# One attention layer and its feed-forward: scores in four 64x64 tiles, and V before the output projection

## What is computed

```python
q = _l2norm(proj(Wq)); k = _l2norm(proj(Wk)); v = proj(Wv)        # 16 heads of 16
attn = einsum('bhqd,bhkd->bhqk', q, k)
mask = (rel < 0) | (rel >= WINDOW)                                # rel = key - query, WINDOW = 128
attn = softmax(attn + where(mask, -1e30, -abs(rel) * slope_of_head))
out  = einsum('bte,de->btd', einsum('bhqk,bhkd->bhqd', attn, v), Wo)
x = _layernorm(x + out)
x = _layernorm(x + ffn(x))         # 256 -> 1024 -> 256, weights binarised per row, exact gelu
```

## Time and profile before

| what | us |
|---|---|
| median of 3 runs | 373.69 (373.42 to 374.68) |
| the profiled execution, its own time | 373.84 |
| its span in the trace | 372.1 |
| TensorE busy | 358.0 (96%) |
| VectorE busy | 318.2 (86%) |
| ScalarE busy | 310.0 (83%) |
| GpSimd busy | 274.5 (74%) |

### The profile page before, as it was taken

How to read it: one execution, slowest core, us unless ns; L and a number is a source line. 1 busy time by engine, 2 the same in 40 slices (tenths; PEclk the granted TensorE clock), 3 DMA queues, 4 the chain that set the end, 5 groups by cost and what they waited for, 6 DMA issues and landing times.

```text
span 372.1 us, 11965 instructions
## 1 busy us (share of the span) xinstructions
PE 358.0 (96%) x3933; PEld 243.9 (66%) x3933; DVE 318.2 (86%) x856; ACT 310.0 (83%) x539; POOL 274.5 (74%) x418
## 2 busy tenths in 40 slices
PE   8699999999999999999999999999999999999991
PEld 5445567766766776676676667775666666666671
DVE  3967789998898988888998997869789999999995
ACT  3579789888898898898899999887888888887873
POOL 1169999899999999999999999857554754754321
PEclk9989999999999999999999999999999999999998
DMA  6757944564464446467676754303303404404113
GB/s 225 147 80 173 193 93 117 105 121 87 111 124 101 111 100 127 100 156 162 132 140 143 160 106 82 58 3 60 58 0 58 114 18 98 114 17 97 58 57 113
DMA packets 99490, 38.31 MB, mean 103 GB/s; under 512 B 84736, under 2 KB 98432, under 8 KB 99328
## 3 DMA queue, kind: packets, MB, share of 16 engines
q1 hardware_dynamic: 99456, 37.89, 46.7%
HBM read 12.72 MB, written 4.19 MB: 45 GB/s over the span
## 4 chain that ended last, share of the span: by engine, by line
PE 62%; DVE 24%; issue 5%; DMA 4%; SPq 2%; ACT 1%; DVEq 1%; POOL 0%; POOLq 0%
PE ps L392 14%; PE ps L402 13%; PE ps L435 9%; PE ps L372 8%; PE ps L411 6%; DVE prob L1150 4%; DVE w L1150 4%; PE ps L532 4%; PE ps L419 3%; DVE zstats L1170 3%; DVE resid L1198 3%; PE ps L566 2%; PE ps L426 2%; DVE z L1160 2%; SPq L273 2%
## 5 line engine op out<-in xcount | busy, mean ns | idle before, releaser
L1363 POOL TENSOR_SCALAR_AFFINE_SELECT prob<-prob 128x512 f32<-128x512 f32 x252 | 154.4, 648 | 14.0 <-ACT prob L673 13.4
L673 ACT ACTIVATE prob<-ps 128x1024 f32<-128x1024 f32 (+1 forms) x128 | 122.2, 1009 | 11.6 <-PE ps L372 11.5
L402 PE MATMUL ps<-wqkv,xt 128*128 128x512 f32 x124 | 60.4, 610 | 1.4 <-DVE qkn L934 1.1
L532 PE MATMUL ps<-yT,sgn 128*128 128x512 f16 x256 | 61.1, 379 | 0.0
L745 ACT ACTIVATE ps<-ps,bias,alpha 128x512 f32<-128x512 f32 x64 | 47.9, 750 | 15.6 <-PE ps L532 12.5
L1431 POOL TENSOR_TENSOR resid<-z,resid 128x256 f32 (+1 forms) x31 | 22.6, 728 | 46.0 <-DVE z L1160 46.0
L392 PE MATMUL ps<-prob,vdiag 128*17 128x128 f32 x1024 | 51.4, 274 | 0.0
L392 PE MATMUL ps<-prob,vnext 128*17 128x128 f32 x992 | 50.0, 273 | 0.0
L372 PE MATMUL ps<-qkT 64*128 64x256 f16 (+1 forms) x512 | 38.8, 270 | 2.1 <-DMA qkT<-parts 2.1
L532 PEld LDWEIGHTS ps<-yT,sgn 128*128 128x128 f16 x256 | 25.0, 98 | 22.6
L435 PE MATMUL ps<-wo,oT 128*128 128x256 f32 x128 | 36.2, 405 | 0.0
(11 more groups left out here) (115 smaller groups left out, 679.8 us busy)
## 6 DMA issues: line engine op xcount, KB each, us to landing
xt<-in_xT SPq DMA_DIRECT2D x32, 128.0 KB, 2.1
resid<-in_x SPq DMA_DIRECT2D x32, 128.0 KB, 2.2
out_dram<-resid SPq DMA_DIRECT2D x7, 512.0 KB, 2.9
w<-in_w2T SPq DMA_DIRECT2D x1, 1024.0 KB, 8.1
w<-in_w1T SPq DMA_DIRECT2D x4, 256.0 KB, 3.3
w_nat<-in_w SPq DMA_DIRECT2D x4, 256.0 KB, 3.6
wqkv<-in_wqkvT SPq DMA_DIRECT2D x3, 256.0 KB, 4.1
qkT<-parts SPq DMA_TRANSPOSE x32, 4.3
```

The lines of the kernel that those rows point to most:

```text
L402: mm = nc.tensor.matmul(ps[:, QK[slot % 2], :], xt[:, slot, k, :], wqkv[:, k, 0:2 * D], start=(k == 0), stop=(k == DC - 1))
L532: mm = nc.tensor.matmul(ps[:, bank, :], sgn1[:, c, P * k:P * k + P], yT[:, par, a, c, :, :], start=(m == 0), stop=(m == 2 * DC - 1))
L673: nc.scalar.activation(to, scored, ACT.Exp, scale=QK_SCALE ** -2).then_inc(exp_done, 1)
L1363: return nc.gpsimd.affine_select(out=at, in_=at, compare_op=ALU.is_ge, fill=0.0, base=-near, pattern=[[0, CH], [1 if near else -1, P]], ch ...
```

## The change

The scores of a chunk were 4 products of 64 rows by 128 keys with 256 queries. They are now 8 products of 64 rows by 64 keys, each with the 192 queries that those keys can be seen by; the parts of PSUM that are never written are zeroed once at the start. For this the queries of two neighbouring blocks must lie side by side, so `qkT` is laid out anew with a fifth place, and every fourth block's queries are transposed a second time by a DMA of half the size. The order of the probability slots changes with it. In the steps 4 to 28 TensorE projects V right after the first scores, and projects the output after q and k. VectorE follows: sums of squares first, then the residual addition and the layer-norm statistics, then the values. ScalarE's logarithm now waits for the layer-norm statistics of the same step (`ln_seed`), where before VectorE's `half<-ss` carried this wait and the statistics stood ahead of it. The first four residual rows are loaded in two pairs, and a few statements at the start of the feed-forward change places (left out below).

```diff
--- before.py
+++ after.py
...
-OWN_AT, NEAR_AT = (0, 4, 1, 5), (2, 3)
+
+OWN_AT, NEAR_AT = (2, 3, 4, 5), (0, 1)
...
-        qkT = sb("qkT", [P, XS, 2 * (H // 2), P], F16)
+
+        qkT = sb("qkT", [P, 2 * (H // 2), XS + 1, P], F16)
...
-                sp.dma_start_transpose(qkT[:, QSLOT[s]],
+                sp.dma_start_transpose(qkT[:, :, s, :],
                                        parts[:, s % 2].rearrange("p h a d -> p (h a d)")).then_inc(qk_in[s % 2], 16)
+                if s == 0 and not (isinstance(n, int) and n == 0):
+                    sp.dma_start_transpose(qkT[:, 0:H // 2, XS, :],
+                                           parts[:, 0, 0:H].rearrange("p h a d -> p (h a d)")).then_inc(again_in, 16)
...
+            for n in range(2):
+                sp.dma_start(resid[:, n, :], x[n]).then_inc(first_resid[0], 16)
             turn_parts(XS, 0)
-            for n in range(XS):
-                sp.dma_start(resid[:, n, :], x[n]).then_inc(first_resid, 16)
+            for n in range(2, XS):
+                sp.dma_start(resid[:, n, :], x[n]).then_inc(first_resid[1], 16)
...
+                queries_at = (slot - 1) * P if slot else (XS - 1) * P
+                windows = ((0, P + P // 2), (P // 2, 2 * P)) if both else ((P, P + P // 2), (P, 2 * P))
                 for t in range(2):
+                    rows_of_queries = qkT[:, 2 * c + t].rearrange("p s q -> p (s q)")
                     for hp in range(2):
                         row = slice(64 * hp, 64 * hp + 64)
-                        queries = qkT[row, first:last + 1:last - first, 2 * c + t, :] if both else qkT[row, here, 2 * c + t, :]
-                        mm = nc.tensor.matmul(ps[:, SC + 2 * (c % 2) + hp, 2 * P * t:2 * P * t + wide],
-                                              qkT[row, here, H // 2 + 2 * c + t, :], queries,
-                                              start=True, stop=True)
+                        for half, (first, last) in enumerate(windows):
+                            keys = slice(P // 2 * half, P // 2 * half + P // 2)
+                            at = queries_at if both else -P
+                            mm = nc.tensor.matmul(ps[keys, SC + 2 * (c % 2) + hp, 2 * P * t + first:2 * P * t + last],
+                                                  qkT[row, H // 2 + 2 * c + t, slot, keys],
+                                                  rows_of_queries[row, at + first:at + last],
+                                                  start=True, stop=True)
                 mm.then_inc(s_done, 1)
...
-            def project_v(n, slot):
+            def project_v(n, slot, added=None):
 
                 count(pe, v_ready, n)
-                count(pe, resid_done, n - 4)
+                count(pe, resid_done, n - 4 if added is None else added)
...
-                if out:
+                full = out and next1 and next3
+                if full:
+                    project_v(i + 1, (slot + 1) % XS, i - 4)
+                elif out:
                     project_out(i - 4, i + 1)
                 if strips:
                     turn_strips(i - 3)
...
+                if full:
+                    project_out(i - 4, i + 1)
                 if before_rows:
                     before_rows()
                 if strips:
                     turn_rows(i - 3)
-                if next1 and next3 and not early:
+                if next1 and next3 and not full and not early:
                     project_v(i + 1, (slot + 1) % XS)
...
             def norm_of(i, next3, ln):
                 base, cols = norm_base(i, next3), norm_columns(next3, ln)
-                if not next3:
+                if ln:
                     act.wait_ge(ln_seed, i - 3)
...
-            def sums_of(n, ln):
+            def sums_of(n):
...
-                if ln:
-                    dve.wait_ge(ln_seed, n - 6)
...
-                if out and next3:
-                    add_output(i - 4)
...
                     y_row(i - 5, prev3)
+                if next3:
+                    sums_of(i + 3)
+                    if out:
+                        add_output(i - 4)
                 if ln:
                     layer_norm(i - 4)
                 if amid:
                     amid()
-                if next3:
-                    sums_of(i + 3, ln)
-                    if not double_first:
-                        fade_values(i + 1, (slot + 1) % XS)
+                if next3 and not double_first:
+                    fade_values(i + 1, (slot + 1) % XS)
...
             nc.vector.memset(ps[:, OT, :], 0.0).then_inc(consts, 1)
+            nc.vector.memset(ps[:, SC:SC + 4, :], 0.0)
...
-            dve.wait_ge(first_resid, 16 * XS)
             step(4, 0, prev_ln=False)
+            dve.wait_ge(first_resid[1], 16 * 2)
```

60 lines of the change are left out of this document (35 added, 25 removed).

## The result

| | before | after |
|---|---|---|
| median us | 373.56 (4 runs, 373.27 to 374.68) | 382.94 (4 runs, 382.64 to 383.26) |
| the profiled execution, span in the trace | 373.84, 372.1 | 383.13, 381.3 |
| TensorE busy | 358.0 (96%) | 354.7 (93%) |
| VectorE busy | 318.2 (86%) | 321.6 (84%) |
| ScalarE busy | 310.0 (83%) | 312.1 (82%) |

The change makes the kernel 2.5% slower: the ratio is 1.0251, 95% interval 1.0226 to 1.0276. The forecast was 377.4 us with a range up to 381.6. The direction came out, the size did not: 9.4 us where 3.7 were expected.

What follows compares the result with a forecast made beforehand. TensorE bounds the kernel before; afterwards a chain through several engines (7.53 us, 7.48 per step with relief) does. 373.84 + 4.7 - 0.7 - 0.3 = 377.5 profiled, median 377.4 us, range 370.0 to 381.6.

Steps and rivals of the forecast that it cites:

- The scores: TensorE's score products, four tiles at a time: 0.08 us less per pair of chunks, 0.16 per step.
- The logarithm's chain: Exps, GpSimd's masks and low halves, `half<-ss`, addition, statistics, logarithm, next exps: closes at 7.53 us, above TensorE's 7.18.
- It stays held: VectorE's `half<-ss` cannot start before 157.33, so it still waits for GpSimd's low-halves instruction of 157.07 to 158.23.
- The second chain: V opens the step and waits for the previous step's values: a stall up to 0.3 us, not counted again.
- The relief of one step in four: GpSimd's low halves come a chunk earlier there: 0 to 0.43 us less in four steps, giving 7.48 per step.
- The wait for `oT`: TensorE's weighted sums wait for ScalarE's copy of the transposed rows: about 0.08 us per step.
- Outside the loop: Scores in seven other steps, counted as 0.7 us less, and paired first residual loads in step 4, 0.3 less.
- rival D: Second transposing DMA arrives late every fourth step by some 0.5 us: +3, total 380.4 us; chance 0.08.
- Rival B: Score tiles' column halves run in turn on TensorE: pair 0.75 us, step 7.68, total 384.8; chance 0.08.
- A: `half<-ss` is not held and runs in 0.18 us: TensorE's 7.18 is the step, total 370.3; chance 0.17.
- C: `half<-ss` is held only on every second step: mean step 7.33 us, total 373.9; chance 0.12.
- The rule against the scores: Skill's minimum of about 25 ns between product starts: 16 products take 0.40 us, not 0.32; gain per pair 0.03.

Runs made afterwards that it cites:

- The square: Changed kernel (382.94 us) against it with V's values made early (375.60), with the logarithm not waiting for layer-norm statistics (380.82), and with both (374.64).
- orders-only kernel: Kernel before with only the change's new orders on TensorE, VectorE and ScalarE, its own 128-key scores kept: 384.88 us, ratio 1.0304.
- scores-only kernel: Changed kernel with the three engines' old orders put back, keeping the small score tiles, their layout and split residual loads: 370.91 us, again 370.92.

## Why the prediction was wrong

- **What bounds: right.** TensorE has no gap before, and the bound became a ring through several engines.
- **The scores: the pair right, the step not.** 0.45 us a pair where 0.54 - 0.08 = 0.46 was forecast. In steps it brought 0.05, not 0.16: TensorE meets the wait for the row outputs earlier.
- **The logarithm's chain: read right, weighed wrong.** Exps to the end of `half<-ss` 5.38 forecast. From the trace, step behind 133.43: exps at 134.58, `half<-ss` ends 139.97, 5.39. From there to the end of `half<-mv` 1.30 (1.23 forecast), 0.12 to the logarithm (0.04), and 1.15 from there to the next exps (0.88). The last is the largest: it is 0.88 to 0.90 in three steps of four and 1.16 or 1.17 in the fourth, 1.00 on the mean, in the kernel before as in the changed one, and the forecast took it from a single step. So this chain is as long as the step, and the forecast of 7.48 was 0.26 a step short. But cutting it gave back 2.1 us of 9.4, and 1.0 once the other was open. It was not the cause of most of the loss. Nor did "It stays held" hold for every order: with V's values early `half<-ss` slips out in one step of four.
- **The second chain: the step that failed.** "A stall of up to 0.3 would fall inside the 0.3 that the first chain leaves anyway, so it is not counted again." The stall was 0.40 and 0.54 in the step shown, some 0.48 on the mean of the 24 steps, and it doesn't fall inside: V waits, so QK, the squares and the sums start later, `half<-ss` starts later and runs into GpSimd's low halves, and the values that the next V needs are later again. I priced one stall with times of the old order and did not follow it round to its own start. Followed round it is 3.33 + 0.73 + 0.72 + 1.30 + 0.68 + 0.06 = 6.82 and the hold, 7.04 with `half<-ss` in 0.22 and 7.97 with it in 1.15. The square puts 6.2 to 7.3 us on it.
- **The relief of one step in four** was forecast at up to 0.43 in four steps. The trace's four steps are 7.87, 7.83, 7.82 and 7.21 us: the relief is there, 0.6 and more, and the other three are longer than the 7.53 of the forecast by 0.3.
- **The wait for `oT`**: 0.08 forecast; from the second scores at 138.34 to the weighted sums at 139.08 are 0.74, less 0.45 for the pair, 0.29; on the mean of the 24 steps 0.61 less 0.45, 0.16.
- **Outside the loop**: -1.0 forecast, -1.7 measured (-2.1 and +0.4). Much of it is not the change. In the profiled execution of the kernel before, the clock fell behind an idle TensorE; windows, TensorE alone, before and after:

```profile
18.50:22.00 3.50, 3.50 (x13) 0.57 0.37 70
```

```profile
18.50:22.00 3.50, 3.44 (x40) 1.00 0.39 73
```

Behind 1.87 us of idle time the granted clock was 0.57 on the mean of that stretch, so most of it at the lower level of 1.2 GHz. The QK projection there took 3.57 us to the next scores; in the orders-only kernel, behind the same 1.87 us of idle time, the clock stayed at 1.00 and it took 1.92. The orders-only kernel, with the old scores and the old loads, then reaches step 5 at 49.22, 1.1 us sooner than the kernel before. It differs between executions, then: the runs of the kernel before have mean granted clocks from 0.988 to 0.997. The changed kernel is idle for 1.43 there. And the scores-only kernel reached step 5 at 48.13 us in one profile and at 49.05 in the other, so the 2.1 us cannot be divided more finely.
- **The second transposing DMA** (rival D) landed in time: 28 of them between 57 and 225 us, from issue to landing

```profile
DMA to landing us min/median/max: 3.4/4.3/5.1
```

and TensorE waited for `qkT` 1.8 us in all, in two waits, of which the one at 17.23 us, ahead of the loop, is 1.43. **Rival B** fell with the pair of 0.45. **A** and **C** needed the hold to vanish or to halve; `half<-ss` takes 0.80 us on the mean of the 24 steps of the changed kernel (median 0.89), 0.54 in the kernel before.
- **The rule against the scores.** "The trace fits it" was a wrong reading. In the kernel before the scores already start in twos, 3 ns apart, on the two tiles: a view of them that ends at 152.16 already has two starts from 152.15 on, and the last line of the earlier trace rows is such a pair. A start every 25 ns is not what that trace shows.

## What to carry to other kernels

When an operation is moved to the head of a step, list what it waits for from the step before, and follow that dependency once round through every engine until it comes back, hold and all: a stall inside a ring is not absorbed by another stall, it moves the other's inputs. Two rings that share a stretch look equally guilty in one trace; cut each alone and both together, and read the square. And a change of several parts is worth splitting before it is judged: here one part gains 0.5 to 0.8% (two series) and the others lose 3%.

## What the hardware showed that I had not expected

- **Products on four 64x64 tiles start closer than 25 ns.** The same pair of scores in the changed kernel, TensorE's timeline cut off at 133.24, at 133.33 and at 133.42, shows 7, 12 and 16 starts:

```profile
133.12 0.36 PE L388 MATMUL ps<-qkT 64*64 64x192 f16 x7
```

```profile
133.12 0.44 PE L388 MATMUL ps<-qkT 64*64 64x192 f16 x12
```

Sixteen starts in less than 0.30 us are under 20 ns each; they come in four groups of four, 3 or 4 ns apart within most of them. The Trainium skill (TensorE: Matmul & The Clock Gate, "Wait — 56ns, not 53.3ns?") says that start to start never drops below about 25 ns; for products on different tiles this trace does not agree, and streaming decides (4 x 192/2.4 GHz = 0.32 us).
- **A load of 64 columns takes longer than one of 128**: 106 ns for 94 (TensorE's weight loads by line, changed kernel and kernel before).

```profile
L388 PEld LDWEIGHTS ps<-qkT x688: 102/106/107, 61.2 to 223.7; 64*64 64x64 f16 x172
```

```profile
L372 PEld LDWEIGHTS ps<-qkT x368: 92/94/96, 57.8 to 223.0; 64*128 64x128 f16 x184
```

The Trainium skill (TensorEngine Tiling (Array Packing), "Tile-to-Partition Mapping") says that column tiling disables fast weight load; the loads fit that, and most of them lie beside products, since the pair is 0.45 and no more.
- **GpSimd's masks hold VectorE's small instructions too, but not all of them**: `half<-ss` took 0.18 alone, 0.64 over a mask of 0.60, 1.15 over the low halves, and the three instructions of the root's round 0.5 to 0.6 each over masks instead of 0.2. But `half<-mv`, one column instead of 32, never grew, though a mask ran beside each of the 24:

```profile
L871 DVE TENSOR_SCALAR half<-mv x24: 153/153/156, 48.1 to 226.3; 128x1 f32<-128x1 f32 x24
L871 DVE TENSOR_SCALAR half<-ss x24: 219/894/1201, 54.3 to 231.9; 128x32 f32<-128x32 f32 x24
```

The Trainium skill (SBUF — State Buffer, "SBUF: two separate sides") calls the port pair that VectorE and GpSimd share an exclusive lock, kept for the whole instruction, for VectorE instructions in a 2-port mode or with two inputs in SBUF. The held ones' ends, 0.04 to 0.06 us behind GpSimd's, agree with a lock; which mode `half<-ss` and `half<-mv` run in no run here shows.
